# Graph layer with residual and layer norm: ScalarE fetches 15 tiles of rows instead of 9, in groups of twelve, and two TensorE picks become gathers

## The reference

```python
def _L0_gnn_ref(H, Xe, id_Xe, M_W, M_b, U_W, U_b):
    features = H[id_Xe[0]]
    M_in = jnp.concatenate([features, Xe], axis=1)
    Y = jax.nn.relu(M_in @ M_W.T + M_b)
    Z = jax.ops.segment_sum(Y, id_Xe[1], num_segments=H.shape[0])
    U_in = jnp.concatenate([H, Z], axis=1)
    H_next = jax.nn.relu(U_in @ U_W.T + U_b)
    return H_next
edge_index = jnp.stack([src, dst])
x = _layernorm(x + _L0_gnn_ref(x, edge_attr_64, edge_index, L0_gnn_M_W, L0_gnn_M_b, L0_gnn_U_W, L0_gnn_U_b), axis=-1)
```

## Time and profile before

| | |
|---|---|
| median of 3 runs | 1639.65 us (1639.28 to 1639.89) |
| profiled execution, its own time | 1641.58 us |
| span of the profile | 1639.7 us |
| TensorE busy | 1596.5 us (97%) |
| VectorE busy | 1332.8 us (81%) |
| GpSimd busy | 1223.9 us (75%) |
| ScalarE busy | 347.5 us (21%) |

### The profile page before, as it was taken

One profiled execution on the slowest core, in us unless ns is written; L12 is line 12 of the kernel. 1 busy time (PEld: TensorE's weight loads), 2 busy tenths in 40 slices (PEclk: granted clock), 3 DMA queues, 4 the chain that ended last, 5 costly groups with the idle time before them and its releaser, 6 DMA issues.

```text
span 1639.7 us, 53864 instructions
## 1 busy us (share of the span) xinstructions
PE 1596.5 (97%) x18182; PEld 1542.8 (94%) x18182; DVE 1332.8 (81%) x1391; ACT 347.5 (21%) x661; POOL 1223.9 (75%) x1303
## 2 busy tenths in 40 slices
PE   5899999999999999999999999999999999999996
PEld 5899999999999999999999999999999999999995
DVE  6788887888887888888888788888788878878874
ACT  4431111212112112211211111211221211212111
POOL 6777777777777777777777777777777777777774
PEclk9999999999999999999999999999999999999998
DMA  8333332323333333333333333323333332323222
GB/s 176 71 72 72 70 79 65 80 64 79 66 79 65 76 75 71 73 66 79 69 74 72 71 73 72 74 69 73 71 72 78 67 78 65 80 65 78 66 59 47
DMA packets 177806, 120.89 MB, mean 74 GB/s; under 512 B 107140, under 2 KB 156018, under 8 KB 177528
## 3 DMA queue, kind: packets, MB, share of 16 engines
q0 software_dynamic: 40992, 42.04, 13.9%
q1 hardware_dynamic: 105754, 56.86, 13.4%
q10 hardware_dynamic: 30782, 18.51, 4.8%
HBM read 114.08 MB, written 3.20 MB: 72 GB/s over the span
## 4 chain that ended last, share of the span: by engine, by line
POOL 74%; issue 24%; PE 1%; DMA 0%; DVE 0%; POOLq 0%; ACT 0%; DVEq 0%
POOL gathered L427 74%; PE p_pick L1076 0%; DMA src_first<-in_src_dram 0%; PE p_edges_T L1076 0%; PE p_bc L1076 0%; DMA gathered<-Y_rows,src_last 0%; POOL Y L457 0%; PE p_pick L1069 0%; DVE Y L881 0%; POOLq L453 0%; PE p_edges_T L1069 0%; PE p_bc L1069 0%; PE p_bc L1032 0%; PE p_messages L1025 0%; DVE total L866 0%
## 5 line engine op out<-in xcount | busy, mean ns | idle before, releaser
L427 POOL DMA_INDIRECT gathered<-Y_rows,src_all x1238 | 1168.2, 944 | 377.6 <-issue 377.6
L1018 PE MATMUL p_pick<-Y_parts,onehot_src 128*128 128x192 bf16 x12397 | 1053.8, 246 | 7.8 <-DVE onehot_src L812 7.4
L1018 PEld LDWEIGHTS p_pick<-Y_parts,onehot_src 128*128 128x128 bf16 x12397 | 1027.6, 98 | 12.6 <-issue 10.5
L812 DVE TENSOR_TENSOR onehot_src<-p_dve,block_start 128x6272 bf16<-128x6272 int16 x253 | 860.5, 3422 | 6.5
L1025 PE MATMUL p_messages<-onehot,messages 128*64 128x72 f32 x3126 | 238.4, 230 | 4.9 <-ACT messages L568 4.9
L796 DVE TENSOR_TENSOR p_messages<-p_messages,gathered 128x512 f32<-128x512 f32 x191 | 133.3, 698 | 132.3 <-DMA gathered<-Y_rows,src_all 111.5
L1025 PEld LDWEIGHTS p_messages<-onehot,messages 128*64 128x64 f32 x3126 | 209.3, 137 | 29.1 <-ACT messages L568 5.9
L1001 PE MATMUL p_messages<-w_edges,edges_T 128*128 128x128 f32 x1564 | 213.3, 280 | 3.7 <-ACT edges_T L548 3.7
L1001 PEld LDWEIGHTS p_messages<-w_edges,edges_T 128*128 128x128 f32 x1564 | 190.9, 192 | 5.1 <-ACT edges_T L548 3.3
L548 ACT COPY edges_T<-p_edges_T 128x512 f32<-128x512 f32 x196 | 114.5, 584 | 379.8 <-PE p_edges_T L983 370.8
L562 ACT ACTIVATE match<-src_spread,minus_node 128x128 int16<-128x128 int32 x190 | 82.9, 436 | 526.8 <-issue 526.8
(11 more groups left out here) (119 smaller groups left out, 199.3 us busy)
## 6 DMA issues: line engine op xcount, KB each, us to landing
row_tile<-Y_rows SPq DMA_DIRECT2D x2560, 0.2 KB
edges<-in_edge_attr_dram SPq DMA_DIRECT2D x190, 192.0 KB
gathered<-Y_rows,src_all POOLq DMA_INDIRECT x1238
slow_tile<-Y_rows ACTq DMA_DIRECT2D x1152, 0.2 KB
edges<-in_edge_attr_dram SPq DMA_DIRECT2D x191, 64.0 KB
src_spread<-in_src_dram ACTq DMA_DIRECT2D x127, 64.0 KB
src_spread<-in_src_dram ACTq DMA_DIRECT2D x63, 128.0 KB
Y_rows<-Y SPq DMA_DIRECT2D x6, 256.0 KB
```

The lines of the kernel that those rows point to most:

```text
L427: nc.gpsimd.indirect_dma_start(out=gathered[c % G][0:parts, j * D:(j + 1) * D], out_offset=None, in_=table, in_offset=bass.IndirectOffsetO ...
L812: nc.vector.tensor_tensor(onehot_src[k % SLOTS][:, :, :], sources.unsqueeze(1).to_broadcast([P, NW, P]), block_start[:, :, :], ALU.is_equa ...
L1018: last = nc.tensor.matmul(p_pick[k % 2][:, 0:3 * D], onehot_src[k % SLOTS][:, b, :], Y_parts[:, b, :], start=(b == 0), stop=(b == NW - 1))
```

## The change

`SLOW_EVERY` goes from 18 to 12 and `SLOW_AT_ONCE` from 8 to 12, so `slow_chunks` are the chunks 26, 38, ... 194, fifteen of them, where they were 38, 56, ... 182, nine. The 128 rows of a tile are issued in 11 chunks (ten groups of 12 and one of 8), starting 13 chunks and ending 3 chunks ahead of the tile's own chunk, where 16 groups of 8 started 18 ahead and also ended 3 ahead. In chunks 96 and 192 there is one picked tile instead of two, and the other is gathered by GpSimd.

```diff
     def picked_tiles(c):
         if not X <= c < NC:
             return []
-        return [TILES - 2, TILES - 1] if c % 3 == 0 else [TILES - 1]
+        return [TILES - 2, TILES - 1] if c % 3 == 0 and c % 96 > 0 else [TILES - 1]
...
-    SLOW_EVERY = 18
-    SLOW_AT_ONCE = 8
+    SLOW_EVERY = 12
+    SLOW_AT_ONCE = 12
+    SLOW_STEPS = -(-P // SLOW_AT_ONCE)
     slow_chunks = list(range(2 * SLOW_EVERY + 2, NC, SLOW_EVERY))
-    slow_steps = {slow_chunks[t] - 1 - s: (t, P - s * SLOW_AT_ONCE - SLOW_AT_ONCE)
-                  for t in range(len(slow_chunks)) for s in range(2, 2 + P // SLOW_AT_ONCE)}
-    slow_steps = {c: (t, r0 + 2 * SLOW_AT_ONCE) for c, (t, r0) in slow_steps.items()}
+    slow_steps = {slow_chunks[t] - 2 - SLOW_STEPS + s: (t, s * SLOW_AT_ONCE, min(P, (s + 1) * SLOW_AT_ONCE))
+                  for t in range(len(slow_chunks)) for s in range(SLOW_STEPS)}
+    assert SLOW_STEPS + 1 <= SLOW_EVERY
...
-            def load_slow(t, r0):
+            def load_slow(t, r0, r1):
...
                 _, ends = nc.values_load_multi_w_load_instructions(
-                    slow_sources[t:t + 1, r0:r0 + SLOW_AT_ONCE], engines=(mybir.EngineType.Activation,), min_val=0,
+                    slow_sources[t:t + 1, r0:r1], engines=(mybir.EngineType.Activation,), min_val=0,
                     max_val=N - 1, skip_runtime_bounds_check_because="the ends of edges are nodes")
-                for r, end in zip(range(r0, r0 + SLOW_AT_ONCE), ends):
+                for r, end in zip(range(r0, r1), ends):
                     act.dma_start(slow_tile[r:r + 1, :], Y_rows[bass.ds(end, 1), :]).then_inc(s_slow_landed, 16)
```

## The result

The changed kernel takes 1635.57 us (median of 7 runs, 1635.23 to 1636.0), the kernel before 1639.89 us on the same chip (7 runs, 1639.28 to 1641.68): a ratio of 0.9972 with a 95% interval from 0.9962 to 0.9982. That is 4.3 us less (3.0 to 6.2 by the interval) where 5.0 were forecast. A later pair on one chip gave 1636.83 against 1640.26 us, 0.9980 (0.9971 to 0.9989): 3.4 us less, 1.8 to 4.8.

A forecast was written before the change was run, and what follows sets the result against it. GpSimd's gather stream was taken as the bound, TensorE close behind; four gathers fewer at 1.2486 us gave −4.99 us, all other terms 0, so 1639.65 − 4.99 = 1634.7 us. Own range 1632.6 to 1636.8 us; 8 in 10 up to 1638.5.

The forecast's parts named there:

- GpSimd sets the pace: GpSimd's gather stream bounds the loop at 1.2486 us a gather; four gathers fewer give −4.99 us.
- Rival D: TensorE sets the pace after all: two picks fewer would give −8.06 us, 1631.6 us; no separate chance, counted with the forecast.
- Two picks take 8.06 us off TensorE and hide: Dropping second picks in chunks 96 and 192 saves TensorE 4.03 us each, while GpSimd's stream ends only 4.99 us earlier.
- The room of TensorE, 11.0 us: What TensorE can lose in the loop before it replaces GpSimd as the bound: 7.97 + 8.06 − 4.99 us.
- Twelve rows, 4.82 us: ScalarE's issue of twelve row fetches after `rectify`, at 0.401 us each; 1.61 us more than eight.
- The round of 6.83 us: ScalarE's own work in a chunk with twelve rows; 0.13 us over TensorE's one-pick chunk, under GpSimd's 8.11 us pace.
- The wait for `s_slow_copied`, 0.3 us: On ScalarE, directly following the copy it waits for, it adds some 0.3 us to one round in twelve, inside the room.
- The lateness of matches: ScalarE's later matches make VectorE late by 2.2 us at most over 165 groups; loss for TensorE taken as 0.
- Rival B: Gain eaten: TensorE or shared DMA engines hand back 1.7 us or more; 1636.4 to 1642.9, say 1638 us; chance 0.15.
- Rival C: ScalarE becomes the bound: with rows at 0.53 us its round is 8.37 us, time 1667 us; chance 0.08, milder form 0.02.
- The end: After the last gathers, TensorE's idle time and lower clock stay about the same: no change, 2.1 us either way.
- The signs of being wrong: GpSimd gather waits, rows above 0.5 us, TensorE waiting for edge copies or messages, VectorE for matches, an earlier lower clock.

The follow-up runs named there:

- the halves: Changed kernel with both picks kept in chunks 96 and 192: 1632.23 us; changed kernel with ScalarE back at nine tiles, eight rows: 1643.05 us; kernel before: 1639.73 us.
- fourteen with the quick loads: Changed kernel with fourteen rows a group, ScalarE loading sixteen source numbers from a multiple of four and using fourteen: 1636.22 us, ratio 0.9976.
- the 1721 us kernel: Changed kernel with fourteen rows in a group in place of twelve, loading fourteen source numbers at a time: 1721.11 us, ratio 1.0501.

## Why the prediction was right, step by step

- **GpSimd sets the pace, 1.2486 us a gather: right.** The spacing, the count and the 5.0 us at the last gather came as worked out, and the halves moved the time by −7.5 us for six gathers less and +3.3 us for two more. Rival D is excluded by the second. The pace is GpSimd's over the whole loop, not in each part of it: up to 690 us TensorE is the fuller engine.
- **Two picks take 8.06 us off TensorE and hide: right, and a loss.** The picks' busy time fell from 1053.8 to 1045.8 us. What I did not draw from my own numbers is that these picks had not been worth dropping: TensorE had 7.97 us of idle time in the loop, enough to follow GpSimd without six gathers. The forecast held for the whole, but the half of it that touches the picks gives 3.3 to 4.5 us back.
- **The room of TensorE, 11.0 us: right in size.** It idles 9.28 us in the loop of the changed kernel; what the missing 1.7 us went into was not separated.
- **Twelve rows, 4.82 us: right** (4.76 us in the timeline above). **The round of 6.83 us: near, with luck in it.** In the 37 rounds of twelve rows in which the match, the edge copy and the next `rectify` follow without a wait for another engine, the median is 6.91 us. I priced the rows but took over the load of their numbers, which takes longer for twelve than for eight: 0.96 us in the changed kernel's line above, where the same load took 0.72 us before. So the first row comes 1.13 us after the start of `rectify`, in place of 0.89; rows a little shorter, and a `rectify` that starts 0.48 us after the start of the edge copy and not 0.59, make up for most of it:

```profile
1553.31 0.60 ACT L569 ACTIVATE messages<-p_messages 128x512 f32<-128x512 f32 x1 [2.96 <-DVE p_messages L797]
...
1554.44 4.76 ACTq L590 DMA_DIRECT2D slow_tile<-Y_rows  x12
```

- **The wait for `s_slow_copied`, 0.3 us: mis-sized.** In the fourteen rounds in which the copy and the first rows of the next tile stand together, the first row comes 1.87 us after the start of `rectify`, 0.74 us more than in the round above. No match that came late stands right behind one of them.

```profile
331.11 0.60 ACT L569 ACTIVATE messages<-p_messages 128x512 f32<-128x512 f32 x1
331.60 0.24 ACT L595 COPY gathered<-slow_tile 128x64 f32<-128x64 f32 x1
332.98 4.83 ACTq L590 DMA_DIRECT2D slow_tile<-Y_rows  x12
```

- **The lateness of matches: mis-sized,** 6.9 us instead of at most 2.2. That the loss for TensorE is 0 was right all the same: without any row the time is the same. Besides the longer load, two things were missing. I looked at each group alone, while a late round makes the next one late: three of the waits (at 839, 1349 and 1422 us) come one round behind another. And my round has no `copy_rows`, which in some rounds stands between `rectify` and the load, and behind a late `rectify` can wait for SP's rows. Three of the five longest waits, 2.76 us of the 6.9, follow such a round; in the last of them the first row comes 2.77 us after the start of `rectify`:

```profile
1560.50 0.60 ACT L569 ACTIVATE messages<-p_messages 128x512 f32<-128x512 f32 x1
1562.14 0.24 ACT L576 COPY gathered<-row_tile 128x64 f32<-128x64 f32 x1 [1.03 <-DMA row_tile<-Y_rows]
1563.27 4.77 ACTq L590 DMA_DIRECT2D slow_tile<-Y_rows  x12
```

- **Rival B, the gain eaten at the shared DMA engines:** out for the most part. The gathers kept their 944 ns and their spacing with 768 more rows fetched by ScalarE, the loop's DMA share stayed 0.32, and six gathers were worth 7.5 us. The Trainium skill ("DMA: Bandwidth & Descriptors", section "Issuing engines are not separate DMA queues") says that starting transfers from several engines saves only the sequencer's time to initiate them, which is usually small beside the transfer. Here the 1.2486 us that each gather takes of GpSimd's time set the pace, so the trace does not agree with "usually small". A small part of the gain may still be handed back, as the point on the end says.
- **Rival C, ScalarE as the bound:** the mechanism is real, its point of decision was put by the wrong pace. I compared the round with GpSimd's 8.11 us a chunk; what gave way first with sixteen rows was TensorE, which waits for edge copies, at 8.71 us a round (the median) against its own 7.99 us, and by 12 us, not by the 27 us that I had put as the rival's price before that run. At twelve rows, and at fourteen with the quick loads, it does not decide.
- **The end: right within its bounds.** The idle time grew by 0.33 us, the lower clock moved by part of a group, and the profiled end got 0.8 us shorter (37.2 us from the last of these gathers to the end of the span before, 36.4 after). The medians gained 0.7 us less than the gathers alone account for, which the interval of the first pair (3.0 to 6.2 us) cannot tell from nothing; the interval of the later pair (1.8 to 4.8 us) ends just short of 5.0. Whether and where something is handed back stays open.
- **The signs of being wrong:** three of those that I had named showed, in small: VectorE's waits for matches, TensorE's waits for edge copies (5.2 us in six places, 3.7 in five before), and a lower clock that begins ahead of the window of chunk 194. None of them decided.

The best version that was run keeps the rows and both picks: 1632.2 us, 0.9955 of the kernel before.

## What to carry to other kernels

When two engines are almost equally full, find the one that never waits and count its instructions: here every one that went was worth its spacing as long as the other engine could follow, and work taken off the other engine was worth nothing. A change made of two parts should be read in two sums; here one part earned 7.5 us and the other gave 3.3 of it back. An engine with long idle times can still hold up others by what is queued behind its new work: compare its whole round, with the loads of its registers, with the average pace of the engines that wait for it, and read the waits of the bounding engine, not those in front of it.

## What the hardware showed that I had not expected

ScalarE's load of source numbers out of one row of SBUF into registers took 0.49 us for four, 0.72 us for eight, 0.96 us for twelve and 1.20 us for sixteen: 0.24 us more for every four. The fourteen of the 1721 us kernel took 1.4 us or 3.2 us: the groups that start at a multiple of 28 numbers (112 bytes) the shorter time, those that start 14 numbers after one the longer. Starting at multiples of four numbers, sixteen loaded again in 1.20 us, and the kernel was 85 us faster. The count of fourteen costs something by itself: the multiples of 28 are multiples of four too, and fourteen numbers from there took 1.41 us, more than sixteen. Whether a start like the slow ones would cost sixteen numbers as much was not run. The Trainium skill ("DMA: Bandwidth & Descriptors", section "Latency and other measured facts") gives about 600 ns as the floor of such a load. ScalarE's loads of two and of eight numbers, 0.66 and 0.72 us, agree; its load of four took 0.49 us and VectorE's 196 loads of one number (L818) took 0.30 us each, both below it, and here the measurement decides.
